# A hybrid transformer layer on eight cores: weight preparation moved into the first FFN, with smaller buffers

## The chip, the cores and the metric

One Trainium2 chip, 8 cores. Each core runs the same program on its own batch element (2048 tokens of width 1024); the cores do not talk to each other. The metric is the device time of the slowest core, in microseconds; smaller is better.

## What is computed

The reference is one layer of four sublayers, each added to its input after a LayerNorm without gain:

```python
x = x + mamba(_layernorm(x))      # D=1024, ED=2048, 16 states, conv of 15 taps
x = x + ffn(_layernorm(x))
x = x + block_attention(_layernorm(x))   # 16 heads, blocks of 64 tokens
x = x + ffn(_layernorm(x))        # the same weights again

def ffn(x, W1, b1, W2, b2, scale):       # H = 4096
    # m1, m2: products of 8 even and 8 odd early tokens (rank-one terms)
    h = x @ W1.T + scale * einsum('bsd,bhd->bsh', x, m1) + b1
    h = gelu(h)
    return h @ W2.T + scale * einsum('bsh,boh->bso', h, m2) + b2
```

W1 is 4096x1024 and W2 1024x4096, both fp32 in HBM. The kernel computes with bf16 copies, transposed so that the contraction lies on the partitions.

## The kernel before

The program is written as five lists of instructions, one for each engine (`te` TensorE, `ve` VectorE, `ac` ScalarE, `gp` GpSimd, `sy` SyncE). `Q.wait` puts a semaphore wait into a list, `inc` a semaphore increment behind an instruction. An engine works through its list in the order in which the Python code emitted it; nothing reorders it. Every operation is recorded through one helper, so the profile gives nearly all instructions line 57; they are told apart by tile. The profile leaves out digits in the names of buffers: `p_wnat`, `p_wnatB`, `p_wstage` and `p_ptp` are `p2_wnat`, `p2_wnatB`, `p2_wstage` and `p2_ptp` of `emit_prep2`.

The stages run one after the other: a prologue that transposes Win and Wout into DRAM scratch, `emit_mamba` (until a barrier on `st`, the semaphore of the writes to `s_x`), `emit_prep2`, `emit_ffn("a")`, `emit_attn`, `emit_ffn("b")`.

`emit_prep2` (from line 362) makes the transposed copies `s_W1T` and `s_W2T`, 32 rows of 128x1024 bf16 each. A row is done by `prep_row`: 8 transposes on TensorE into `p_ptp` (PSUM), one ScalarE copy into `p_wstage`, one SyncE DMA of 256 KB to DRAM. `p_ptp` and `p_wstage` have two slots, so row ci waits for the copy and the write of row ci-2. For W1, GpSimd loads a row of 128x1024 into one of two slots of `p_wnat`, once the transposes of row i-2 are done; these loads change fp32 to bf16 on the way. For W2, GpSimd issues 8 loads of 128x4096 into `p_wnatB` (64 KB of each partition), the tensor engine waits for all eight (`te.wait(lnb)`), and 32 rows follow. At the end SyncE waits for the last writes of both slots.

`emit_ln` loads four 128x1024 tiles through the two slots of `xres` (SyncE), takes the statistics on VectorE with a square root on ScalarE, normalizes into `xntok`, transposes on TensorE and copies into `xn_fm`.

`emit_ffn` first has SyncE issue 32 loads that bring all of `s_W2T` into SBUF (`f_w2a`, in the second FFN `f_w2b`; 64 KB of each partition), then `emit_ln` for the first quarter of the tokens. The tokens go in four quarters h. For h = 0, eight groups of transposes into `pRow` make the rows `ev1` and `ev4` for the rank-one terms. Then for each of 32 chunks c of H: SyncE loads `f_w1` (three slots) from `s_W1T`, 8 matmuls over the contraction and one of the rank-one term into `pA`, GELU on ScalarE into `f_h`. GpSimd carries small rows (`f_ufl`, `f_vfl`) from partitions 0 to 3 to partition 0. Then four tiles of 128 tokens are multiplied with `f_w2` (this is the first use of it, `te.wait(l_w2)`), and VectorE adds b2 and the residual, through `f_tx`.

The prologue has a relative of the W2 part, `prepB` for Wout: 8 loads of 128x2048 into `wnatB`, then rows with one PSUM tile `p_tp`, so that TensorE waits for ScalarE in every row. Its W1-like part loads Win into two slots `wnat`.

Of the kernel before, what the change touches and what calls it, by code (L numbers as in the profile page):

```python
# [7 lines left out]
F32 = mybir.dt.float32  # L8
BF16 = mybir.dt.bfloat16
# [4 lines left out]
D = 1024  # L14
# [92 lines left out]
def build_program(T=2048, nsub=4):  # L107
# [3 lines left out]
    nc = bass.Bass("TRN2", target_bir_lowering=False)  # L111
# [63 lines left out]
    b2_bc = b.sb("b2_bc", [128, D], F32)  # L175
# [187 lines left out]
    def emit_prep2():  # L363
        with contextlib.ExitStack() as prep:
            pb = lambda n, s, d: prep.enter_context(nc.sbuf_tensor(n, list(s), d))
            pps = lambda n, s, d: prep.enter_context(nc.psum_tensor(n, list(s), d))
            wnat = pb("p2_wnat", [128, 2, 1024], BF16)
            wnatB = pb("p2_wnatB", [128, 8, 4096], BF16)
            wstage = pb("p2_wstage", [128, 2, 1024], BF16)
            p_tp = pps("p2_ptp", [128, 2, 1024], BF16)  # L370
            ltp0 = b.sem("p2ltp0"); ltp1 = b.sem("p2ltp1"); ltpp = (ltp0, ltp1)
            lnb = b.sem("p2lnb")
            ttp = b.sem("p2ttp"); etp = b.sem("p2etp")
            wtp0 = b.sem("p2wtp0"); wtp1 = b.sem("p2wtp1"); wtpp = (wtp0, wtp1)
            tt_toks = []; et_toks = []; wb_toks = []

            def prep_row(ci, in_tile, cache_row):
                sl = ci % 2
                if ci >= 2:
                    te.wait(etp, et_toks[ci - 2])  # L380
                tok = None
                for k in range(8):
                    tok = te.transpose(out=p_tp[:, sl, k * 128:(k + 1) * 128],
                                       in_=in_tile[k],
                                       identity=eye[:, :])
                tok.inc(ttp, 8)
                tt_toks.append(ttp.n)
                ac.wait(ttp, tt_toks[ci])
                if ci >= 2:
                    ac.wait(wtpp[sl], wb_toks[ci - 2][1])  # L390
                ac.activation(out=wstage[:, sl, :], in_=p_tp[:, sl, :],
                              func=AF.Copy).inc(etp, 1)
                et_toks.append(etp.n)
                sy.wait(etp, et_toks[ci])
                sy.dma_start(out=cache_row, in_=wstage[:, sl, :]).inc(wtpp[sl], 16)
                wb_toks.append((wtpp[sl], wtpp[sl].n))

            ci = 0
            for i in range(32):
                sl = i % 2  # L400
                if i >= 2:
                    gp.wait(ttp, tt_toks[i - 2])
                gp.dma_start(out=wnat[:, sl, :],
                             in_=h_W1[i * 128:(i + 1) * 128, :]).inc(ltpp[sl], 16)
                te.wait(ltpp[sl])
                prep_row(ci, [wnat[:, sl, k * 128:(k + 1) * 128] for k in range(8)],
                         s_W1T[i, :, :])
                ci += 1
            for k in range(8):
                gp.dma_start(out=wnatB[:, k, :],  # L410
                             in_=h_W2[k * 128:(k + 1) * 128, :]).inc(lnb, 16)
            te.wait(lnb)
            for j in range(32):
                prep_row(ci, [wnatB[:, k, j * 128:(j + 1) * 128] for k in range(8)],
                         s_W2T[j, :, :])
                ci += 1
        return (wtp0, wtp1)

    def emit_ln(xsrc, tiles, xn_fm, kind, lnps_bf):
        for j, i in enumerate(tiles):  # L420
# [40 lines left out]
            if j == 0:  # L461
                te.wait(l_cv)
                te.wait(l_ox, l_ox.n)
            tok = None
            for k in range(8):
                tok = te.transpose(out=lnps_bf[:, k * 128:(k + 1) * 128],
# [360 lines left out]
                wout(h)  # L827
            barrier(st)

    def emit_ffn(tag, is_last):  # L830
        THF = T // 4
        NTHF = NT // 4
        fch = [(s0, min(512, THF - s0)) for s0 in range(0, THF, 512)]
        with contextlib.ExitStack() as fs:
# [9 lines left out]
            vfl = fb("f_vfl" + tag, [1, 16 * THF], BF16)  # L844
            vsb = fb("f_vsb" + tag, [4, THF], BF16)
            usb = fb("f_usb" + tag, [4, THF], BF16)
            ftx = fb("f_tx" + tag, [128, D], F32)
            pA = fs.enter_context(nc.psum_tensor("f_pA" + tag, [128, 2, 1024], F32))
            pR = fs.enter_context(nc.psum_tensor("f_pR" + tag, [4, 1024], F32))
            pRow = fs.enter_context(nc.psum_tensor("f_pRow" + tag, [1, 1024], BF16))  # L850
            pLN = fs.enter_context(nc.psum_tensor("f_pLN" + tag, [128, 1024], BF16))

            for k in range(32):
                sy.dma_start(out=w2a[:, k, :], in_=s_W2T[k, :, :]).inc(l_w2, 16)

            W1TOK = {}
            w1sem = (s_wzp[0], s_wzp[1], s_wzz[0])
            l_ev = emit_ln(s_x, list(range(NTHF)), xn_fm[:, 0, :, :], "plain", pLN[:, :])
            lntok = {0: l_ev.n}
            for h in range(4):  # L860
                xh = xn_fm[:, h % 2, :, :]
                te.wait(l_ev, lntok[h])
# [36 lines left out]
                for c in range(32):  # L899
                    sl = c % 2  # L900
                    sl3 = c % 3
                    if c >= 3:
                        sy.wait(s_q3, W1TOK[c - 3])
                    sy.dma_start(out=w1s[:, sl3, :], in_=s_W1T[c, :, :]).inc(w1sem[sl3], 16)
                    te.wait(w1sem[sl3])
                    if c >= 2:
                        te.wait(l_h, l_h.n - 1)
                    tok = None
                    for k in range(8):
                        for (t0, tw) in fch:  # L910
                            tok = te.matmul(out=pA[:, sl, t0:t0 + tw],
                                            lhsT=w1s[:, sl3, k * 128:(k + 1) * 128],
                                            rhs=xh[:, k, t0:t0 + tw],
                                            start=(k == 0), stop=False)
                    if c == 0:
                        te.wait(lg, lg.n)
                    ii = c // 8
                    for ti, (t0, tw) in enumerate(fch):
                        tok = te.matmul(out=pA[:, sl, t0:t0 + tw],
                                        lhsT=ev1[0:1, ii * 1024 + (c % 8) * 128:ii * 1024 + (c % 8) * 128 + 128],  # L920
                                        rhs=ufl[0:1, ii * THF + t0:ii * THF + t0 + tw],
                                        start=False, stop=True)
                    tok.inc(s_q3, 1)
                    W1TOK[c] = s_q3.n
                    ac.wait(s_q3)
                    ac.activation(out=hT[:, c, :], in_=pA[:, sl, 0:THF], func=AF.Gelu,
                                  bias=b1_fm[:, c:c + 1]).inc(l_h, 1)
                    if c % 8 == 7:
                        qi = c // 8
                        if qi == 0:  # L930
                            te.wait(s_q1, s_q1.n)
                        else:
                            te.wait(lg, lg.n)
                        te.wait(l_h, l_h.n)
                        tok = None
                        for k in range(8):
                            for (t0, tw) in fch:
                                tok = te.matmul(out=pR[:, t0:t0 + tw],
                                                lhsT=ltc[:, k, 9:16:2],
                                                rhs=hT[:, qi * 8 + k, t0:t0 + tw],  # L940
                                                start=(k == 0), stop=(k == 7))
                        tok.inc(l_v, 1)
                        ac.wait(l_v)
                        if qi >= 1:
                            ac.wait(lg, lg.n)
                        ac.activation(out=vsb[:, 0:THF], in_=pR[:, 0:THF],
                                      func=AF.Copy).inc(s_q4, 1)
                        gp.wait(s_q4)
                        for ii2 in range(4):
                            gp.dma_start(out=vfl[0:1, (qi * 4 + ii2) * THF:(qi * 4 + ii2 + 1) * THF],  # L950
                                         in_=vsb[ii2:ii2 + 1, 0:THF]).inc(lg, 16)
# [6 lines left out]
                for tt in range(NTHF):  # L958
# [13 lines left out]
                    for ii in range(4):  # L972
                        for qi in range(4):
# [3 lines left out]
                                            start=False, stop=(qi == 3 and ii % 2 == 1))  # L977
                    tok.inc(l_o, 1)
                    ve.wait(l_o); ve.wait(lxrp[sl])
                    ve.tensor_add(out=ftx[:, :], in0=xres[:, sl, :], in1=b2_bc[:, :])  # L980
                    ve.dr()
                    ve.tensor_add(out=xres[:, sl, :], in0=ftx[:, :],
                                  in1=pA[:, sl, 0:1024]).inc(l_ox, 1)
                    xr_used(sl, l_ox)
                    sy.wait(l_ox)
# [189 lines left out]
                barrier(st)  # L1175

    emit_mamba()
    p2sems = emit_prep2()
    sy.wait(p2sems[0]); sy.wait(p2sems[1])
    if nsub >= 2:  # L1180
        emit_ffn("a", is_last=(nsub == 2))
    if nsub >= 3:
        emit_attn()
    if nsub >= 4:
# [57 lines left out]
```

How the kernel before makes its waits and increments, by code:

```python
    def inc(self, sem, k=1):  # L41
        sem.n += k
        box = self.box
        self.q.rec.append(lambda e: box["i"].then_inc(sem.h, k))
        return self
# [21 lines left out]
    def wait(self, sem, n=None):  # L67
        v = sem.n if n is None else n
        if v > 0:
            self.rec.append(lambda e, v=v: e.wait_ge(sem.h, v))
```

## Time and profile before

| | us |
|---|---|
| median of 3 runs | 5758.94 |
| lowest and highest | 5660.82, 5759.61 |
| the profiled execution | 5649.85 |
| its span on the slowest core (core 3) | 5648.3 |
| spans of the 8 cores | 5614.4 to 5648.3 |

| engine | busy us | share of the span |
|---|---|---|
| PE (matmul) | 2743.2 | 49% |
| DVE (VectorE) | 2548.4 | 45% |
| ACT (ScalarE) | 1755.7 | 31% |
| POOL (GpSimd) | 399.9 | 7% |

The shares are averages over stages with different limits: the Mamba stage (until about 3291 us) is bound by the scans on VectorE, the two FFN (about 3577 to 4297 and 4924 to 5648 us) by TensorE. The mean granted clock of TensorE is 0.725 to 0.729 on all cores. In the rows below, a time is in microseconds from the first instruction, "x8" is the number of instructions merged into a row, and the brackets hold the idle time of the engine before it and what ended it. Landing is the time from the issue of a DMA to its semaphore.

### The profile page before, as it was taken

How to read it: one execution, taken by the hardware profiler on the slowest of the kernel's cores; microseconds unless marked ns; L12 is line 12 of the kernel's file. 1: busy time of each engine (PE TensorE's matmuls, PEld its weight loads, DVE VectorE, ACT ScalarE, POOL GpSimd, SP SyncE). 2: the span in 40 equal slices, each digit the busy share in tenths (PEclk: the TensorE clock that was granted, in tenths of full speed). 3: DMA queues.
4: the chain of work that ended last, by engine and by line, in shares of the span. 5: the costliest groups of instructions: out<-in, count | busy, mean ns of one | idle time of the engine just before them, and what ended most of it. 6: DMA issues, size and time to landing. Idle time of an engine off the chain costs nothing.

```text
span 5648.3 us, 41604 instructions; the slowest of 8 cores (5614.4 to 5648.3 us)
## 1 busy us (share of the span) xinstructions
PE 2743.2 (49%) x12960; PEld 1202.1 (21%) x12960; DVE 2548.4 (45%) x2198; ACT 1755.7 (31%) x2562; POOL 399.9 (7%) x378
## 2 busy tenths in 40 slices
PE   3352333323333233332222322698896544398988
PEld 2220111101111111111000111233332322233333
DVE  0106999249996299990999610101101333210010
ACT  2213555125553055540555322311111222212111
POOL 1140111001110001110000010000000000000000
PEclk9985666666666666666565755888997666588889
DMA  7412000320001400004000167322224111322221
GB/s 118 102 38 43 19 19 19 52 80 19 19 21 25 112 13 20 19 16 97 20 12 14 56 131 186 97 73 73 83 75 93 58 62 56 119 75 90 84 73 64
DMA packets 202301, 345.40 MB, mean 61 GB/s; under 512 B 49924, under 2 KB 86916, under 8 KB 201060
## 3 DMA queue, kind: packets, MB, share of 16 engines
q1 hardware_dynamic: 173990, 289.47, 17.8%
q0 software_dynamic: 28096, 53.27, 5.6%
q8 instruction: 109, 1.79, 0.1%
q14 instruction: 106, 0.87, 0.1%
HBM read 301.06 MB, written 71.45 MB: 66 GB/s over the span
## 4 chain that ended last, share of the span: by engine, by line
PE 33%; DVE 27%; issue 10%; DMA 10%; DVEq 8%; ACT 5%; SPq 5%; POOL 1%; another core or an unknown queue 1%; ACTq 0%; POOLq 0%
DVE m_hall L57 15%; PE f_pAb L57 11%; PE f_pAa L57 10%; DVEq L73 8%; DVE m_dBall L57 5%; SPq L57 5%; PE a_pA L57 3%; PE m_pB L57 3%; DVE m_txd L57 2%; DMA m_yfr<-s_yfc 2%; DMA xres<-x 1%; DMA p_wnat<-W 1%; PE m_pA L57 1%; POOL m_diag L57 1%; DMA xres<-s_x 1%
## 5 line engine op out<-in xcount | busy, mean ns | idle before, releaser
L57 DVE TENSOR_TENSOR_SCAN m_hall<-m_dA,carry,m_dBall 128x512 bf16<-128x512 f32 x1024 | 1342.8, 1385 | 11.9 <-issue 11.0
L57 PE MATMUL m_pB<-m_gall,eye 128*128 128x512 bf16 x1024 | 365.4, 535 | 1428.8 <-DVE m_gall L57 1428.8
L57 ACT ACTIVATE m_dA<-m_delta,A_fm 128x512 f32<-128x512 f32 x1024 | 731.9, 721 | 949.8 <-DVE m_hall L57 854.2
L57 DVE BATCH_NORM_STATS2 stat<-xres 128x6 f32<-128x512 f32 x128 | 82.0, 683 | 1073.7 <-DMA xres<-s_x 854.5
L57 PEld LDWEIGHTS m_pB<-m_gall,eye 128*128 128x128 bf16 x1024 | 128.0, 129 | 1654.6 <-issue 1626.0
L57 ACT ACT_TABLE_LOAD x158 | 202.7, 1283 | 768.0 <-DVE r1a L57 387.9
L57 POOL TENSOR_TENSOR m_diag<-convw_fm,eye 128x1920 bf16<-128x1920 f32 x64 | 240.4, 3756 | 1417.2 <-PE m_pB L57 1417.2
L57 DVE TENSOR_TENSOR m_dBall<-m_dxb,m_bcB 128x8192 bf16<-128x8192 bf16 x64 | 283.2, 4425 | 5.9
L57 DVE TENSOR_TENSOR m_gall<-m_hall,m_bcC 128x8192 bf16<-128x8192 bf16 x64 | 283.2, 4425 | 0.6 <-issue 0.6
L57 PE MATMUL f_pAb<-f_w2b,f_hb 128*128 128x512 bf16 x1024 | 258.1, 419 | 4.5 <-DMA f_vflb<-f_vsbb 4.5
L57 PE MATMUL f_pAb<-f_xnb,f_w1b 128*128 128x512 bf16 x1024 | 253.1, 392 | 9.6 <-DMA f_w1b<-s_W1T 9.6
L57 PE MATMUL f_pAa<-f_xna,f_w1a 128*128 128x512 bf16 x1024 | 251.6, 390 | 10.6 <-DMA f_w1a<-s_W1T 10.5
L57 PE MATMUL f_pAa<-f_w2a,f_ha 128*128 128x512 bf16 x1024 | 251.2, 411 | 4.5 <-DMA f_vfla<-f_vsba 4.5
L57 PE MATMUL m_pB<-m_xinp,m_diag 128*128 128x512 bf16 x960 | 230.6, 394 | 46.0 <-POOL m_diag L57 46.0
L57 DVE TENSOR_SCALAR m_txd<-xres,mu,r1a 128x1024 f32<-128x1024 f32 x16 | 16.5, 1033 | 492.0 <-DMA xres<-x 367.4
L57 DVE TENSOR_TENSOR f_txb<-xres,b_bc 128x1024 f32<-128x1024 f32 x16 | 19.6, 1226 | 381.7 <-PE f_pAb L57 381.7
L57 DVE TENSOR_TENSOR f_txa<-xres,b_bc 128x1024 f32<-128x1024 f32 x16 | 19.6, 1226 | 374.9 <-PE f_pAa L57 374.9
L57 PE MATMUL m_pA<-m_wouta,m_yfr 128*128 128x512 bf16 x256 | 72.4, 409 | 230.7 <-DMA m_yfr<-s_yfc 230.3
L57 ACT ACTIVATE f_ha<-f_pAa,b_fm 128x512 bf16<-128x512 f32 x128 | 87.9, 687 | 181.4 <-PE f_pAa L57 181.4
L57 ACT ACTIVATE f_hb<-f_pAb,b_fm 128x512 bf16<-128x512 f32 x128 | 87.9, 687 | 181.3 <-PE f_pAb L57 181.3
L57 ACT ACTIVATE p_wstage<-p_ptp 128x1024 bf16<-128x1024 bf16 x64 | 64.7, 1023 | 248.6 <-PE p_ptp L57 231.7
L57 PEld LDWEIGHTS f_pAb<-f_w2b,f_hb 128*128 128x128 bf16 x1024 | 107.7, 106 | 153.1 <-issue 55.7
(154 smaller groups left out, 3456.5 us busy)
## 6 DMA issues: line engine op xcount, KB each, us to landing
xres<-s_x SPq DMA_DIRECT2D x96, 512.0 KB, 3.3
f_w1a<-s_W1T SPq DMA_DIRECT2D x128, 256.0 KB, 2.6
f_w1b<-s_W1T SPq DMA_DIRECT2D x128, 256.0 KB, 2.6
s_x<-xres SPq DMA_DIRECT2D x48, 512.0 KB
xres<-x SPq DMA_DIRECT2D x32, 512.0 KB, 3.7
m_wz<-s_WinT POOLq DMA_DIRECT2D x64, 256.0 KB, 2.9
m_wzz<-s_WinT SPq DMA_DIRECT2D x64, 256.0 KB, 2.7
m_wouta<-s_WoutT SPq DMA_DIRECT2D x64, 256.0 KB, 2.6
```

Source lines behind the costliest of these rows:

```text
L57: box["i"] = getattr(e, fname)(*a, **kw)
L73: self.rec.append(lambda e: e.drain())
```

## The change

- `emit_prep2` is no longer called between the stages. `emit_ffn("a")` calls it as `prep_hook`, after its first `emit_ln` has been emitted. To let it live beside the FFN's buffers it is made smaller: one slot of `p_wnat`, `p_wnatB` of 512 columns, one slot of `p_ptp`.
- A row now waits for the copy of the row before, and a W1 load for the transposes of the row before. W2 goes in eight pieces: 8 loads of 128x512, then 4 rows; the loads of a piece wait for the last transposes before it.
- The loads of `f_w2` move from SyncE, ahead of `emit_ln`, to GpSimd, behind `emit_ln` and the hook; in the first FFN each waits for the write of its row. The second FFN has no hook. SyncE waits for each W1 row before it loads it, for h = 0.
- `pRow` becomes a part of `pLN`, with a wait on `s_q1` in `emit_ln`; `f_tx` goes, the sum is formed in `xres`.

```diff
-            wnat = pb("p2_wnat", [128, 2, 1024], BF16)
-            wnatB = pb("p2_wnatB", [128, 8, 4096], BF16)
+            wnat = pb("p2_wnat", [128, 1, 1024], BF16)
+            wnatB = pb("p2_wnatB", [128, 8, 512], BF16)
...
-            p_tp = pps("p2_ptp", [128, 2, 1024], BF16)
+            p_tp = pps("p2_ptp", [128, 1024], BF16)
...
-                if ci >= 2:
-                    te.wait(etp, et_toks[ci - 2])
+                if ci >= 1:
+                    te.wait(etp, et_toks[ci - 1])
...
-                if i >= 2:
-                    gp.wait(ttp, tt_toks[i - 2])
-                gp.dma_start(out=wnat[:, sl, :],
+                if i >= 1:
+                    gp.wait(ttp, tt_toks[i - 1])
+                gp.dma_start(out=wnat[:, 0, :],
...
-            for k in range(8):
-                gp.dma_start(out=wnatB[:, k, :],
-                             in_=h_W2[k * 128:(k + 1) * 128, :]).inc(lnb, 16)
-            te.wait(lnb)
-            for j in range(32):
...
+            for quar in range(8):
+                gp.wait(ttp, tt_toks[ci - 1])
+                for k in range(8):
+                    gp.dma_start(out=wnatB[:, k, :],
+                                 in_=h_W2[k * 128:(k + 1) * 128,
+                                          quar * 512:(quar + 1) * 512]).inc(lnb, 16)
+                te.wait(lnb, lnb.n)
+                for j in range(4):
...
+        return (wb_toks[0:32], wb_toks[32:64])
...
                 te.wait(l_ox, l_ox.n)
+                te.wait(s_q1, s_q1.n)
...
-            ftx = fb("f_tx" + tag, [128, D], F32)
...
-            pRow = fs.enter_context(nc.psum_tensor("f_pRow" + tag, [1, 1024], BF16))
             pLN = fs.enter_context(nc.psum_tensor("f_pLN" + tag, [128, 1024], BF16))
-
-            for k in range(32):
-                sy.dma_start(out=w2a[:, k, :], in_=s_W2T[k, :, :]).inc(l_w2, 16)
+            pRow = pLN[0:1, :]
...
             lntok = {0: l_ev.n}
+            ptoks = prep_hook() if prep_hook is not None else None
+            for k in range(32):
+                if ptoks is not None:
+                    gp.wait(ptoks[1][k][0], ptoks[1][k][1])
+                gp.dma_start(out=w2a[:, k, :], in_=s_W2T[k, :, :]).inc(l_w2, 16)
...
                         sy.wait(s_q3, W1TOK[c - 3])
+                    if ptoks is not None and h == 0:
+                        sy.wait(ptoks[0][c][0], ptoks[0][c][1])
...
-                    ve.tensor_add(out=ftx[:, :], in0=xres[:, sl, :], in1=b2_bc[:, :])
+                    ve.tensor_add(out=xres[:, sl, :], in0=xres[:, sl, :], in1=b2_bc[:, :])
...
-    p2sems = emit_prep2()
-    sy.wait(p2sems[0]); sy.wait(p2sems[1])
     if nsub >= 2:
-        emit_ffn("a", is_last=(nsub == 2))
+        emit_ffn("a", is_last=(nsub == 2), prep_hook=emit_prep2)
```

## Rows read from the trace of the kernel before

**Rows 1.** The page: span; granted TensorE clock in 40 slices (tenths)

```profile
span 5648.3 us, 41604 instructions; the slowest of 8 cores (5614.4 to 5648.3 us)
...
PEclk9985666666666666666565755888997666588889
```

**Rows 2.** Windows: start:end, length, busy us (instructions) PE, PEld, DVE, ACT, POOL; PEclk, DMA share, GB/s

```profile
3291.00:3402.00 111.00, 32.38 (x256) 24.77 (x256) 0.00 (x0) 31.71 (x31) 21.02 (x40) 0.50 0.79 152
3402.00:3449.00 47.00, 0.00 (x0) 0.00 (x0) 0.00 (x0) 1.02 (x1) 0.00 (x0) 0.50 0.99 177
...
3505.00:3554.00 49.00, 4.05 (x32) 3.10 (x32) 10.69 (x29) 5.85 (x9) 0.00 (x0) 0.50 0.69 231
...
3577.00:3675.00 98.00, 80.17 (x353) 30.88 (x352) 10.62 (x28) 31.06 (x46) 9.72 (x20) 0.93 0.34 105
```

**Rows 3.** Chain that ended last: start us, length us, what held it

```profile
3401.01 48.13 another core or an unknown queue
3524.86 10.93 DMA xres<-s_x
```

**Rows 4.** Timeline, W1 rows: start us, us, engine, operation [idle before <-releaser]

```profile
3290.81 1.12 POOL L57 DMA_DIRECT2D p_wnat<-W  x2 [748.53 <-DMA s_x<-xres]
...
3302.44 1.01 PE L57 MATMUL p_ptp<-eye,p_wnat 128*128 128x128 bf16 x8 [4.50 <-DMA p_wnat<-W]
...
3304.00 0.53 POOL L57 DMA_DIRECT2D p_wnat<-W  x1 [4.98 <-PE p_ptp L57]
```

**Rows 5.** Landing of the p_wnat loads, issue to landing

```profile
DMA to landing us min/median/max: 4.3/4.7/6.6
```

**Rows 6.** The same for the loads wnat of the first weight (Win)

```profile
DMA to landing us min/median/max: 4.4/4.5/6.9
```

**Rows 7.** The same for POOL loads without type change (m_wz, 256 KB)

```profile
DMA to landing us min/median/max: 2.7/2.9/5.0
```

**Rows 8.** POOL queue, 3300 to 3390 us: packets, MB, share of 16 engines

```profile
q0 software_dynamic: 3886, 7.08, 59.8%
```

**Rows 9.** The same, 3405 to 3448 us (W2 load)

```profile
q0 software_dynamic: 1016, 7.35, 98.5%
```

**Rows 10.** The same, 158 to 184 us (Wout load)

```profile
q0 software_dynamic: 1102, 4.03, 99.0%
```

**Rows 11.** Timeline of POOL: the Wout load is issued

```profile
153.78 4.23 POOL L57 DMA_DIRECT2D wnatB<-Wout  x8 [6.39 <-PE p_tp L57]
```

**Rows 12.** Timeline of the Wout rows (one PSUM buffer)

```profile
185.36 1.01 PE L57 MATMUL p_tp<-eye,wnatB 128*128 128x128 bf16 x8 [29.64 <-DMA wnatB<-Wout]
...
187.69 1.01 PE L57 MATMUL p_tp<-eye,wnatB 128*128 128x128 bf16 x8 [1.32 <-ACT wstage L57]
```

**Rows 13.** Timeline of the W2 rows (two PSUM buffers)

```profile
3449.38 1.87 PE L57 MATMUL p_ptp<-eye,p_wnatB 128*128 128x128 bf16 x16 [48.37 <-DMA p_wnatB<-W]
...
3454.90 1.93 PE L57 MATMUL p_ptp<-eye,p_wnatB 128*128 128x128 bf16 x16 [1.27 <-ACT p_wstage L57]
```

**Rows 14.** Timeline, start of the first FFN

```profile
3505.32 19.39 SPq L57 DMA_DIRECT2D f_w2a<-s_W2T  x32
...
3535.89 1.29 DVE L57 BATCH_NORM_STATS2 stat<-xres 128x6 f32<-128x512 f32 x2 [248.32 <-DMA xres<-s_x]
...
3551.61 1.01 PE L57 MATMUL f_pLNa<-eye,xntok 128*128 128x128 bf16 x8 [2.45 <-DVE xntok L57]
...
3554.29 1.01 PE L57 MATMUL f_pRowa<-eye,f_ltca 128*1 128x128 bf16 x8 [1.67 <-DVE f_ltca L57]
```

**Rows 15.** Timeline, start of the second FFN

```profile
4848.07 20.27 SPq L57 DMA_DIRECT2D f_w2b<-s_W2T  x32
4868.50 19.18 SPq L57 DMA_DIRECT2D xres<-s_x  x4
4879.05 1.29 DVE L57 BATCH_NORM_STATS2 stat<-xres 128x6 f32<-128x512 f32 x2 [33.73 <-DMA xres<-s_x]
```

**Rows 16.** The page, part 6: issues, KB each, median us to landing

```profile
xres<-s_x SPq DMA_DIRECT2D x96, 512.0 KB, 3.3
```

More of the change, by code:

```diff
@@ L378, in prep_row @@
                 sl = ci % 2
-                if ci >= 2:
-                    te.wait(etp, et_toks[ci - 2])
+                if ci >= 1:
+                    te.wait(etp, et_toks[ci - 1])
                 tok = None
                 for k in range(8):
-                    tok = te.transpose(out=p_tp[:, sl, k * 128:(k + 1) * 128],
+                    tok = te.transpose(out=p_tp[:, k * 128:(k + 1) * 128],
                                        in_=in_tile[k],
@@ L390, in prep_row @@
                     ac.wait(wtpp[sl], wb_toks[ci - 2][1])
-                ac.activation(out=wstage[:, sl, :], in_=p_tp[:, sl, :],
+                ac.activation(out=wstage[:, sl, :], in_=p_tp[:, :],
                               func=AF.Copy).inc(etp, 1)
@@ L399, in emit_prep2 @@
             for i in range(32):
-                sl = i % 2
-                if i >= 2:
-                    gp.wait(ttp, tt_toks[i - 2])
-                gp.dma_start(out=wnat[:, sl, :],
-                             in_=h_W1[i * 128:(i + 1) * 128, :]).inc(ltpp[sl], 16)
-                te.wait(ltpp[sl])
-                prep_row(ci, [wnat[:, sl, k * 128:(k + 1) * 128] for k in range(8)],
+                if i >= 1:
+                    gp.wait(ttp, tt_toks[i - 1])
+                gp.dma_start(out=wnat[:, 0, :],
+                             in_=h_W1[i * 128:(i + 1) * 128, :]).inc(ltpp[i % 2], 16)
+                te.wait(ltpp[i % 2])
+                prep_row(ci, [wnat[:, 0, k * 128:(k + 1) * 128] for k in range(8)],
                          s_W1T[i, :, :])
                 ci += 1
-            for k in range(8):
-                gp.dma_start(out=wnatB[:, k, :],
-                             in_=h_W2[k * 128:(k + 1) * 128, :]).inc(lnb, 16)
-            te.wait(lnb)
-            for j in range(32):
[L414 to L417, printed above, removed]
+            for quar in range(8):
[6 more added lines that the diff above has]
+                for j in range(4):
+                    prep_row(ci, [wnatB[:, k, j * 128:(j + 1) * 128] for k in range(8)],
+                             s_W2T[quar * 4 + j, :, :])
+                    ci += 1
+        return (wb_toks[0:32], wb_toks[32:64])
     def emit_ln(xsrc, tiles, xn_fm, kind, lnps_bf):
@@ L828, in emit_mamba, with emit_ffn @@
             barrier(st)
-    def emit_ffn(tag, is_last):
+    def emit_ffn(tag, is_last, prep_hook=None):
         THF = T // 4
@@ L979, in emit_ffn @@
                     ve.wait(l_o); ve.wait(lxrp[sl])
-                    ve.tensor_add(out=ftx[:, :], in0=xres[:, sl, :], in1=b2_bc[:, :])
+                    ve.tensor_add(out=xres[:, sl, :], in0=xres[:, sl, :], in1=b2_bc[:, :])
                     ve.dr()
-                    ve.tensor_add(out=xres[:, sl, :], in0=ftx[:, :],
+                    ve.tensor_add(out=xres[:, sl, :], in0=xres[:, sl, :],
                                   in1=pA[:, sl, 0:1024]).inc(l_ox, 1)
@@ L1177, in build_program @@
     emit_mamba()
-    p2sems = emit_prep2()
-    sy.wait(p2sems[0]); sy.wait(p2sems[1])
     if nsub >= 2:
-        emit_ffn("a", is_last=(nsub == 2))
+        emit_ffn("a", is_last=(nsub == 2), prep_hook=emit_prep2)
+    else:
+        emit_prep2()
     if nsub >= 3:
```

## The prediction, made before the changed kernel was timed

> **What bounds the kernel now.** I read the page first: the busy shares of the engines, the granted clock by slice and the chain, which show a program of stages one after the other. The change touches none of the scans of the Mamba stage and none of the FFN's matrix loops; it touches the passage between them, 3290 to 3577 us, and the start of the second FFN, from 4848 us. In the passage TensorE runs at its lower level, 1.2 GHz (PEclk 0.50), and idles more than it works; in the FFN it is granted 0.93 [rows 1, 2]. So I asked the windows, the chain and the timeline of that passage what each row waits for.
>
> Three things bound it. In the W1 part PE is busy 32.4 of 111 us and the DMA engines 0.79: each row of W1 waits for its load [rows 2]. Then all of W2 is loaded in one piece; the chain holds it as one step of 48.1 us, with the DMA engines at 0.99 [rows 2, 3]. The 32 W2 rows that follow go in pairs, four of them in 3454.90 - 3449.38 = 5.5 us [rows 13]. At last SP issues 32 loads of f_w2a in 19.4 us before it issues the first load of the LayerNorm, which then takes 10.9 us to land behind them [rows 3, 14]. From POOL's first W1 load (3290.81) to the first transpose into pRow (3554.29) it is 263.5 us [rows 4, 14]. I predict this stretch anew, and the start of the second FFN.
>
> **The change part by part.**
>
> *Order.* The hook stands in emit_ffn, but each engine runs its own list in order. PE gets the 4 LayerNorm groups, then all 64 rows of prep, then the first FFN's work; ACT and SP likewise. No FFN matmul can run under prep. What can overlap is one W1 load with the LayerNorm, and the w2a loads with the end of prep.
>
> *LayerNorm first, +20.4 us ahead of prep.* Its load is issued at about 3290.8, when the barrier opens, and lands in 3.3 us [rows 16]; from the first statistics to the fourth group of transposes it is 3551.61 - 3535.89 = 15.7 us [rows 14]; its 8 transposes take 1.0 us. 3.3 + 15.7 + 1.0 = 20.0, with 0.4 for issue. Row 0 of W1 begins at 3311.2; its load, issued at 3290.8, is hidden under this.
>
> *W1 with one wnat buffer.* The next load may be issued only when the row's transposes are done. From the start of a row's transposes to the load that they release it is 3304.00 - 3302.44 = 1.56 us [rows 4]. The load took 4.3 / 4.7 / 6.6 us with mostly two in flight [rows 5], 4.4 / 4.5 / 6.9 for Win, where loads overlap less [rows 6]. Now one is in flight alone: I take 4.4, and 0.1 until PE starts. Period 6.1 us (5.95 at the minimum; 6.9 at 5.2). 31 periods are 189.1 us, so the last row starts at 3500.3. The SP write-back and the ACT copy of a row end inside 6.1 us, so the single PSUM buffer costs nothing here.
>
> *W2 rows with one PSUM buffer.* PE must wait for ACT after each row. The Wout rows of the prologue have just this form: 187.69 - 185.36 = 2.33 us a row [rows 12]. Four rows start within 3 x 2.33 = 7.0 us.
>
> *W2 in eight pieces.* Each piece is 8 loads of 128x512, 1 MB as bf16 against 8 MB before, and its issue waits until the last transpose of the piece before. So nothing of it is hidden. No row shows such a piece; I bound it. By bytes: one 256 KB load lands in 4.5 us [rows 6], the Wout load, 8 x 512 KB, took from 153.78 to 185.36, 31.6 us [rows 11, 12]; the line through both gives 1 MB at 9.9. By packets: POOL's queue used 90 x 16 x 0.598 / 3886 = 222 ns of an engine for a packet of W1 (2 KB runs), 43 x 16 x 0.985 / 1016 = 667 ns for W2 (8 KB), 26 x 16 x 0.99 / 1102 = 374 ns for Wout (4 KB) [rows 8, 9, 10]. Halving the run takes off 293, then 152 ns, next perhaps 76: 146 ns for the new 1 KB runs. A piece has 1024 of them and 128 small ones, 72 for each engine: 10.5 us, and 2.5 us of start and end (4.5 less nine packets of 222 ns), together 13.0. I take 12, nearer to packets. Lower end 8.5 (W2's own rate, 5.9 us per MB, and 2.5); upper end 18 (1 KB runs cost what 2 KB runs do, 72 x 222 ns = 16.0, and 2.5, rounded). A piece then takes 1.56 + 12 + 7.0 = 20.6 us, eight take 164.5, and the last row starts at 3664.8. PE is free for pRow 1.0 us later, at 3665.8, against 3554.3: +111.5 us. From there the first FFN runs as before.
>
> *w2a on POOL.* 32 issues, 0.58 us each at most, of which 28 can go out under the last piece's transfers and rows; POOL is done at about 3669 and is next wanted for f_ufl at about 3690. That is the cover; if it fails, f_ufl waits some us. In the first FFN the 19.4 us of SP issue and the slow LayerNorm load are thus gone, which the sum above holds already, since nothing of them stands in it.
>
> *Second FFN, gain.* Its LayerNorm load is issued at 4868.50, behind 20.3 us of w2b issues, and DVE starts at 4879.05 [rows 15]. Now both start at 4848.1 on two queues. The bounds: DVE starts 3.3 us later if the load is undisturbed (27.5 us gained), or the load fares as if behind the w2b stream (0). The DMA engines share, and the later LayerNorm loads meet the stream too: I take 22.
> The page "DMA: Bandwidth & Descriptors" of the Trainium skill (Issuing engines are not separate DMA queues) says that a second issuing engine saves only the time on the sequencer. By that the gain is the 20.3 us of issue; the sum would be 2 us higher.
>
> *At nothing:* pRow as a part of pLN with its wait on s_q1 (the count is reached when xntok is), the add into xres instead of ftx (the same shape), and the waits of SP on write-backs long landed. Clock: PE idles longer, at the level it already has.
>
> **Sum.** +111.5 - 22 = +89.5 us on the profiled execution, 5649.85 us by its own time (span 5648.3): 5739 us, 1.6% more. The median of the runs shown is 5758.94, 109 us above that execution, their lowest 5660.82: the same sum on the median is 5848, one more reason for a high upper end.
>
> A rule that speaks otherwise: the Trainium skill, "DMA: Bandwidth & Descriptors" (Anatomy of one DMA), puts a POOL load at about 2.0 us and its bytes over 436 GB/s. For 256 KB that is 2.6 us; this trace has at least 4.3 [rows 5], so it disagrees for these loads, which change type on the way. By the Trainium skill's page W1 would take 31 x 4.3 us and a piece about 6, and the kernel would end near 5634.
>
> **The rivals.**
> A, the pieces are dear (slower by over 2%). The 1 KB runs cost nearly what the 2 KB runs do. From 15 us a piece the total passes 5763 (+24 us in eight pieces). For it: the price of a packet falls more slowly than its bytes at each halving [rows 8 to 10]; eight starts and ends. Against: it falls at each. At 17 us: 5779; with lone loads of 5.2 us as well: about 5800.
> B, a lone load is quick (not slower, the other side). The 4.5 us might be mostly a queue of two. POOL's plain loads of 256 KB landed in 2.9 us [rows 7]. Then W1's period is 4.56 and takes 141.4; a piece takes 3.7 of issue and 2.9, 6.6, eight 121.3. 20.4 + 141.4 + 121.3 + 1.0 = 284.1, +20.6, less 22: 5648. It decides from about 3 us a load. Against: the minimum of 64 loads that change type is 4.3 us [rows 5, 6].
> The formula of the Trainium skill's page "DMA: Bandwidth & Descriptors" (Anatomy of one DMA) amounts to much the same.
> C, prep is hidden under the FFN after all. Then over 200 us go, 5430. The order of PE's list forbids it.
>
> **How the numbers follow.** Forecast (about +90, 5700 to 5790): 0.60. A: 0.28. B: 0.09. C: 0.03. The low end of the forecast is 4.3 us a load, 8.5 a piece and 27.5 gained: 5701. The high ends together (5.2, 18, no gain) give 5834. The range 5690 to 5850 leaves out B, C and a little on top. Over 2% or not is about what a measurement can tell: faster 0.03 (C), within 2% (below 5763) 0.65 (most of the forecast, and B), slower 0.32 (A and the forecast's upper part).
>
> **What would show it.** In the profile after: the W1 rows of p_ptp 6.1 us apart, with POOL released by PE in each; eight waits of PE for p_wnatB, about 12 us each, where one of 48 us stood; rows 2.33 us apart between them; the passage from barrier to pRow about 375 us long; w2a issued from POOL with no wait on the path; DVE of the second FFN at about 4854 on the old time scale. Wrong would be: loads under 3.5 us, pieces over 15 us or under 8, FFN matmuls between prep rows, f_ufl late behind w2a, or another clock in the FFN.

## The result, and the profile after

| | before | after |
|---|---|---|
| median of all executions (10 and 10) | 5671.03 us | 5819.35 us |
| lowest, highest | 5635.53, 5782.31 us | 5736.12, 5876.94 us |
| the profiled execution | 5649.85 us | 5744.98 us |
| its span | 5648.3 us | 5743.4 us |

The ratio of after to before is 1.0181, with a 95% interval of 1.012 to 1.0242: the change made the kernel slower by about 1.8%, and the interval leaves open whether it is more than 2%. The executions of either kernel lie on two levels some 100 us apart, whatever the kernel, so the ratio is taken between executions on the lower level, and the medians of the table, which mix the two, say less.

The page of the kernel after, its span and the granted clock:

```profile
span 5743.4 us, 41755 instructions; the slowest of 8 cores (5696.7 to 5743.4 us)
...
PEclk9985666656666666666666655689897667698888
```

After the prologue the clock stands at 5 and 6 tenths until the first FFN, much as before (5 to 7 tenths [rows 1]); only the FFN begins later.

The W1 rows in the timeline of the kernel after (start us, us, engine, operation, idle time before it and what ended it):

```profile
3313.29 1.06 PE L57 MATMUL p_ptp<-eye,p_wnat 128*128 128x128 bf16 x8
...
3319.84 1.01 PE L57 MATMUL p_ptp<-eye,p_wnat 128*128 128x128 bf16 x8 [5.49 <-DMA p_wnat<-W]
...
3321.39 0.53 POOL L57 DMA_DIRECT2D p_wnat<-W  x1 [5.96 <-PE p_ptp L57]
...
3325.99 1.01 PE L57 MATMUL p_ptp<-eye,p_wnat 128*128 128x128 bf16 x8 [5.14 <-DMA p_wnat<-W]
...
3327.54 0.53 POOL L57 DMA_DIRECT2D p_wnat<-W  x1 [5.62 <-PE p_ptp L57]
```

A row every 6.2 us, and POOL waits 5.6 us for PE before each load: load and transposes take turns. Before, two loads were in flight, and POOL was held for the row before the last [rows 4]. The landing of these loads, from the tile's view:

```profile
DMA to landing us min/median/max: 4.2/4.4/7.6
```

The median is 4.4 us alone against 4.7 with two in flight [rows 5].

The W2 part in the chain that ended last (start us, length us, what):

```profile
3508.63 3.64 POOL p_wnatB L57 x7
3512.27 6.07 DMA p_wnatB<-W
...
3645.86 9.04 DMA p_wnatB<-W
3659.74 7.70 DMA s_W2T<-p_wstage
```

Where one load of 48.1 us stood in the chain [rows 3], there are eight issues of 3 to 4 us with 5 to 9 us of landing behind each. Two pieces and the end of prep in the timeline (PEld is the weight load of TensorE; the last row is the first transpose of pRow):

```profile
3518.58 1.01 PE L57 MATMUL p_ptp<-eye,p_wnatB 128*128 128x128 bf16 x8 [10.50 <-DMA p_wnatB<-W]
...
3520.91 1.01 PE L57 MATMUL p_ptp<-eye,p_wnatB 128*128 128x128 bf16 x8 [1.32 <-ACT p_wstage L57]
...
3537.53 1.01 PE L57 MATMUL p_ptp<-eye,p_wnatB 128*128 128x128 bf16 x8 [10.94 <-DMA p_wnatB<-W]
...
3646.39 14.96 POOL L57 DMA_DIRECT2D f_w2a<-s_W2T  x28
...
3655.15 1.01 PE L57 MATMUL p_ptp<-eye,p_wnatB 128*128 128x128 bf16 x8 [13.47 <-DMA p_wnatB<-W]
...
3665.04 1.02 ACT L57 ACTIVATE p_wstage<-p_ptp 128x1024 bf16<-128x1024 bf16 x1 [5.37 <-DMA s_W2T<-p_wstage]
...
3667.15 0.72 PEld L57 LDWEIGHTS f_pLNa<-eye,f_ltca 128*1 128x1 bf16 x8 [0.20 <-issue]
```

The first piece took 3518.58 - 3508.63 = 9.95 us, the rows come 2.33 us apart, as in the Wout part [rows 12]. The last piece took 12.9 us (3655.15 - 3642.22, its first issue), because POOL sends 28 loads of f_w2a right behind it (3646.39); they also hold up a write-back, for which ACT waits 5.4 us at 3665.04.

The start of the second FFN:

```profile
4962.63 14.25 SPq L57 DMA_DIRECT2D xres<-s_x  x4
4963.01 6.96 POOL L57 DMA_DIRECT2D f_w2b<-s_W2T  x13 [546.66 <-DMA s_x<-xres]
4968.03 1.29 DVE L57 BATCH_NORM_STATS2 stat<-xres 128x6 f32<-128x512 f32 x2 [8.27 <-DMA xres<-s_x]
...
4991.70 1.01 PE L57 MATMUL f_pLNb<-eye,f_ltcb 128*1 128x128 bf16 x8 [1.67 <-DVE f_ltcb L57]
```

SP and POOL start within 0.4 us, VectorE follows 5.4 us after the issue of its load, and pRow is reached after 4991.70 - 4962.63 = 29.1 us, where it was 49.4 us (4848.07 to 4897.47; the start is in [rows 15]).

The difference of the two profiled executions, 95.1 us of span, is made up so: the passage, from POOL's first W1 load to pRow, is 3667.15 - 3291.40 = 375.8 us against 263.5, +112.3; the second FFN's start -20.3; everything else +3.1.

### The profile page after: what moved, and what is told of

Same layout as the page of the kernel before. It is cut to its first block, busy times and chain, and to the rows that moved or that the text cites. A ratio compares the mean times of both kernels' runs of the same rounds, so it can differ in the third digit from the quotient of the medians.

```text
span 5743.4 us, 41755 instructions; the slowest of 8 cores (5696.7 to 5743.4 us)
## 1 busy us (share of the span) xinstructions
PE 2736.9 (48%) x12960; PEld 1199.9 (21%) x12960; DVE 2548.3 (44%) x2198; ACT 1756.9 (31%) x2562; POOL 462.2 (8%) x498
## 4 chain that ended last, share of the span: by engine, by line
PE 33%; DVE 27%; DMA 11%; issue 11%; DVEq 8%; ACT 5%; SPq 4%; POOL 2%; ACTq 0%; POOLq 0%
DVE m_hall L57 15%; PE f_pAb L57 10%; PE f_pAa L57 10%; DVEq L73 7%; DVE m_dBall L57 5%; SPq L57 4%; PE a_pA L57 3%; PE m_pB L57 3%; DMA p_wnat<-W 2%; DVE m_txd L57 2%; DMA m_yfr<-s_yfc 2%; DMA xres<-x 1%; PE m_pA L57 1%; PE p_ptp L57 1%; POOL m_diag L57 1%
## 5 line engine op out<-in xcount | busy, mean ns | idle before, releaser
L57 DVE TENSOR_TENSOR xres<-xres,b_bc 128x1024 f32<-128x1024 f32 x32 | 39.2, 1225 | 757.1 <-PE f_pAa L57 379.4
L57 PEld LDWEIGHTS f_pAa<-f_w2a,f_ha 128*128 128x128 bf16 x1024 | 106.7, 105 | 150.0 <-issue 50.4
```

Of the source, the lines that this page charges most:

```text
L57: box["i"] = getattr(e, fname)(*a, **kw)
```

## The experiments

Each of the runs below is read by its trace: the passage by stages, with the stretch from the first to the last transpose of PE for W1, from there to the last transpose for W2, and to pRow. Before these are 105, 100 and 53 us, after they are 194, 159 and 0.3 (the LayerNorm, 20 to 22 us, now stands in front).

**One slot of p_wnat, alone**, in the kernel before.

```diff
-            wnat = pb("p2_wnat", [128, 2, 1024], BF16)
+            wnat = pb("p2_wnat", [128, 1, 1024], BF16)
...
-                if i >= 2:
-                    gp.wait(ttp, tt_toks[i - 2])
+                if i >= 1:
+                    gp.wait(ttp, tt_toks[i - 1])
...
```

> The kernel before with one slot of p_wnat and nothing else changed. Theory (costs add, each wait is serial): the W1 rows come 6.2 us apart where they came 3.4 apart, 31 periods are 89 us more, the W2 part is unchanged; the profiled time is about 5739. Rival (the loss of the change comes from prep standing behind the LayerNorm in the first FFN, not from its buffers): the W1 rows stay under 4 us apart and the time is within 20 us of before.

The tile p_ptp: engine, operation, count, durations, first and last start:

```profile
L57 PE MATMUL p_ptp<-eye,p_wnat x256: 263/311/314, 3299.6 to 3494.8; 128*128 128x128 bf16 x128
```

195 us for 31 periods: the whole loss of the W1 part comes from this slot, wherever prep stands. The passage was 358.2 us, 95 more. The time was 5745.4 us, 96 above before on the same chip (5649.63; one execution of each).

**One slot of p_ptp, alone.**

```diff
-            p_tp = pps("p2_ptp", [128, 2, 1024], BF16)
+            p_tp = pps("p2_ptp", [128, 1024], BF16)
...
-                if ci >= 2:
-                    te.wait(etp, et_toks[ci - 2])
+                if ci >= 1:
+                    te.wait(etp, et_toks[ci - 1])
...
```

> The kernel before with one slot of p_ptp. Theory: nothing in the W1 part, whose rows wait for loads; the W2 rows go from 1.6 to 2.33 us apart, 31 of them are +21.5 us; about 5671. Rival (PE waits for ACT in the W1 part too): the W1 rows lengthen by up to 1 us each, 30 us more.

```profile
L57 PE MATMUL p_ptp<-eye,p_wnat x256: 263/311/314, 3302.6 to 3409.0; 128*128 128x128 bf16 x128
...
L57 PE MATMUL p_ptp<-eye,p_wnatB x256: 265/314/314, 3458.8 to 3533.6; 128*128 128x128 bf16 x128
```

The W1 rows take 106 us, as before; the W2 rows take 74.8 us from first to last start, where they took 51.4 (3449.4 to 3500.8). +23 us there, and the passage is 288.7 us, +25. Of its two times, 5676.2 and 5835.3 us, the profiled one is the lower. The rival on the W1 part is out.

**Eight pieces, alone**, with both slots of p_ptp.

```diff
-            wnatB = pb("p2_wnatB", [128, 8, 4096], BF16)
+            wnatB = pb("p2_wnatB", [128, 8, 512], BF16)
...
+            for quar in range(8):
+                gp.wait(ttp, tt_toks[ci - 1])
...
```

> The kernel before with W2 in eight pieces, two slots of p_ptp kept. Theory: a piece is 1.6 us until its issue, 10.4 us of load and 3.5 us until its fourth row starts, 15.5 in all, 124 us for eight where 100 stood: +24, about 5674. The rival that the pieces are dear because of their short runs: loads of 15 us or more, +60 us.

```profile
3397.79 4.24 POOL L57 DMA_DIRECT2D p_wnatB<-W  x8 [6.72 <-PE p_ptp L57]
...
3409.14 1.86 PE L57 MATMUL p_ptp<-eye,p_wnatB 128*128 128x128 bf16 x16 [11.90 <-DMA p_wnatB<-W]
...
3413.95 4.24 POOL L57 DMA_DIRECT2D p_wnatB<-W  x8 [11.92 <-PE p_ptp L57]
...
3424.20 1.86 PE L57 MATMUL p_ptp<-eye,p_wnatB 128*128 128x128 bf16 x16 [10.79 <-DMA p_wnatB<-W]
```

Pieces of 11.4 and 10.3 us, 15.1 us from piece to piece (3424.20 - 3409.14); the last W2 row starts 125 us after the last W1 row, against 100. The time was 5668.6, +19. A piece isn't dear: my rival A falls.

**The loads of f_w2 on POOL, alone**: the gaining half of the change, in the kernel before.

```diff
             for k in range(32):
-                sy.dma_start(out=w2a[:, k, :], in_=s_W2T[k, :, :]).inc(l_w2, 16)
+                gp.dma_start(out=w2a[:, k, :], in_=s_W2T[k, :, :]).inc(l_w2, 16)
...
     sy.wait(p2sems[0]); sy.wait(p2sems[1])
+    gp.wait(p2sems[0]); gp.wait(p2sems[1])
```

> The kernel before with the 32 loads of f_w2 issued by POOL, in both FFN (in the first POOL waits for the last write-backs first). Theory: this is the gaining half of the change: 20 us at the second FFN as in the changed kernel, and about 20 at the first, where VectorE starts the LayerNorm some 5 us after the issue where it took 30, and the LayerNorm runs 5 us longer beside the stream; about 5610. Rival (the DMA engines are shared, so nothing is gained at the first FFN): 20 us in all, 5630.

Its three executions took 5720.7, 5760.6 and 5813.9 us where 5610 was expected, so the time of this run shows no gain. In the profiled one cores 4 and 5 had a granted clock of 0.71, where before has 0.725 to 0.729 on all cores; I read core 3, at 0.729, whose span was 5598.3 us. Start of the first FFN there:

```profile
3502.73 13.52 SPq L57 DMA_DIRECT2D xres<-s_x  x4
3503.09 4.81 POOL L57 DMA_DIRECT2D f_w2a<-s_W2T  x9 [109.02 <-DMA s_W2T<-p_wstage]
3507.19 1.29 DVE L57 BATCH_NORM_STATS2 stat<-xres 128x6 f32<-128x512 f32 x2 [223.61 <-DMA xres<-s_x]
```

VectorE starts 4.5 us after the issue of its load, where it started 30.6 us after SP's first w2a issue [rows 14]; from the last W2 row to pRow it is 33.6 us against 53.5, and the second FFN's start takes 28.9 against 49.4. Together 40 us in the stretches that the loads stand in. Timed by itself:

> The kernel before with the loads of f_w2 on POOL, timed. The undisturbed cores of its profile were 40 to 45 us shorter than before: the theory expects a ratio of 0.992 to 0.994. Rival: no gain, 1.00.

The ratio was 0.9979, interval 0.9935 to 1.0023: about 12 us, less than expected. No gain at all is not excluded by it, but 40 us on the slowest core are just outside (the interval ends at 37). The typical core did gain: in the executions behind the ratio the median of the eight cores was 5592.5 to 5609.7 us, where it was 5629.2 to 5651.6 before, some 35 us less. In the trace of this run both stretches are short again on every core that I read, but on its slowest core, core 6, the last stretch from pRow took 762.8 us, where core 3 of before took 750.8; from the second matrix phase on, the products with f_w2b, the granted clock was 0.86 there against 0.88. Why the slowest core gives back most of the 40 us is open; in the kernel after, where the same loads were moved, that stretch stayed level (751.7).

**Two slots of p_wnat in the kernel after.**

```diff
-            wnat = pb("p2_wnat", [128, 1, 1024], BF16)
+            wnat = pb("p2_wnat", [128, 2, 1024], BF16)
...
-                if i >= 1:
-                    gp.wait(ttp, tt_toks[i - 1])
+                if i >= 2:
+                    gp.wait(ttp, tt_toks[i - 2])
...
```

> The changed kernel with two slots of p_wnat, which undoes that one part. Theory: the W1 rows return to 3.4 us apart, -88 us: about 5655, level with before. Rival (placement costs): a gain under 40 us.

The first execution profiled had TensorE at 0.70 on all cores and took 5823.5 us, far from the 5655 expected; its passage was 284.5 us, 91 less. It was repeated:

> The changed kernel with two slots of p_wnat once more, since the execution profiled before ran at a lower clock in all its stages outside prep. Theory: the passage is 285 us as then, the rest as in the changed kernel, about 5655. Rival: the quicker passage is paid back in the FFN or the attention, over 5700.

```profile
L57 PE MATMUL p_ptp<-eye,p_wnat x256: 262/311/314, 3313.5 to 3417.5; 128*128 128x128 bf16 x128
...
L57 PE MATMUL p_ptp<-eye,p_wnatB x256: 262/314/314, 3428.5 to 3577.7; 128*128 128x128 bf16 x128
```

104 us of W1 rows, a passage of 284.7 us and a time of 5658.8: 86 us less than after, and level with before: the passage is 21.2 us longer than before, and the second FFN's start 20.4 us shorter (4907.9 - 4878.9 = 29.0). So the place of prep, the pieces and the single p_ptp cost, together, no more than the moved loads give back; the 90 us of this slot are the loss that is seen.

**What a lone load is made of.**

```diff
-                             in_=h_W1[i * 128:(i + 1) * 128, :]).inc(ltpp[i % 2], 16)
+                             in_=s_WinT[i, :, :]).inc(ltpp[i % 2], 16)
```

> The changed kernel, with the W1 rows read from the bf16 scratch of Win instead of from W1, so the load keeps its type and reads half the bytes; the FFN is so computed with other weights. Theory (the time of a lone load is its transfer with change of type on top of a start): a load lands in 2.9 us as m_wz did, the rows come 4.6 us apart, -51 us: about 5694. Rival (a lone load costs 4.4 us whatever it carries, start and end): 6.2 us apart, no change.

```profile
L57 PE MATMUL p_ptp<-eye,p_wnat x256: 263/311/314, 3311.7 to 3469.1; 128*128 128x128 bf16 x128
...
DMA to landing us min/median/max: 2.9/3.3/4.8
```

The load of bf16 rows, half the bytes and no change of type, lands in 3.3 us, and the rows come 157.4 / 31 = 5.1 us apart, not 4.6. The time was 5709.2 us, 36 less than after, where the theory had 51 and the rival nothing. I had carried 2.9 us over from m_wz and was 0.4 short; the theory holds in kind, but most of a lone load's time is left when the bytes are halved. Of the 6.2 us of a period about 1.1 are the other half of the bytes and the change of type, 3.3 what even this load takes, 1.6 the transposes and the way back to POOL.

**f_w2a held back.**

```diff
                 if ptoks is not None:
-                    gp.wait(ptoks[1][k][0], ptoks[1][k][1])
+                    gp.wait(ptoks[1][30][0], ptoks[1][30][1])
+                    gp.wait(ptoks[1][31][0], ptoks[1][31][1])
```

> The changed kernel with the f_w2a loads held back until the last two write-backs of prep have landed. Theory (the stream of w2a slows the last piece and the last write-backs): the last piece loads in 10.4 us where it took 12.9, and the 5 us stall of ScalarE before the last but one row goes; 5 to 7 us less in the passage. Rival (they are then in the way of f_ufl and f_w1a): as much is lost after it; the sum is within 3 us.

PE's waits on core 0 of this run, between 3640 and 3780 us (us in total, times, longest):

```profile
PE f_pAa L57 <- DMA f_ufla<-f_usba: 7.8, 1, 7.8
...
PE p_ptp L57 <- ACT p_wstage L57: 4.0, 3, 1.3
```

The stall of ACT is gone, the last piece took 10.3 us on core 6 where it took 12.9, and the passage is 3.2 to 8.3 us shorter (367.5 to 370.3 against 373.5 to 375.8, cores 6 and 0 against 3 and 1). But f_ufl now queues behind f_w2a on POOL's queue, and PE waits 7.8 us for it (11.4 on core 6), where it waited 2.5; the stretch from the first product with f_w1a to the second matrix phase takes 106.0 and 110.1 us on cores 0 and 6, where it took 98.4 and 99.9 on cores 1 and 3 of after. In its first 20 us the granted clock was 0.81 and 0.63, where it was 1.00 and 0.87. The rival was right: it is paid back, and somewhat more. The time was even 5765.4 us, 20 above after; most of that lies behind the second matrix phase, on core 6 at a mean granted clock of 0.719, and no run explains it. This is the cover that the prediction named, a few us wide.

**Two pieces instead of eight**, into the free buffer f_ha.

```diff
-            for quar in range(8):
+            for quar in range(2):
...
-                    gp.dma_start(out=wnatB[:, k, :],
+                    gp.dma_start(out=hT[:, 4 * k:4 * k + 4, :].rearrange("p a b -> p (a b)"),
...
-                                          quar * 512:(quar + 1) * 512]).inc(lnb, 16)
+                                          quar * 2048:(quar + 1) * 2048]).inc(lnb, 16)
```

> The changed kernel with W2 loaded in two pieces of 2048 columns, into the buffer f_ha, which is free during prep. Theory: a piece is now 4 MB with runs of 4 KB and takes between 26 and 31.6 us (the Wout load); the W2 part is 2 x (1.6 + 26 to 31.6 + 35) = 125 to 136 us where 152 to 159 stood: -15 to -30 us. If a piece of 1 MB was mostly start and end (7 us or more of its 10.4), the gain is over 35 us.

```profile
3513.31 3.64 POOL f_ha L57 x7
3516.95 25.72 DMA f_ha<-W
3579.47 2.99 POOL f_ha L57 x6
3583.11 26.45 DMA f_ha<-W
```

A piece of 4 MB takes 29.4 us (3.64 + 25.72), four times the bytes for 2.8 times the time of a piece of 1 MB. The stretch from the last W1 to the last W2 row is 138.8 us, 20 less, within what was expected. The time was 5727.95.

**Prep inside the first quarter of the first FFN.** The runs say that the loss is serial waiting for loads while PE works 32 us in each part and the DMA engines are half idle (shares of 0.47 and 0.59 in the W1 and W2 parts of the kernel after). The remedy is to have loads in flight under work that must be done anyway.

```diff
                 for c in range(32):
...
+                    if inl:
+                        if c + 1 < 32:
+                            row1(c + 1)
+                        te.wait(et1, E1[c])
...
+                    if inl:
+                        row2(c)
```

`row1` has the 8 transposes of a W1 row, the copy into its slot of f_w1, the write to s_W1T and the load of the row four further on; between it and `row2` stand the matmuls and the GELU of chunk c; `row2` transposes a W2 row into pLN, copies it into f_w2a and writes s_W2T. The buffers of this version: four slots of p_wnat, two pieces of W2 (one of its own, one in the second half of f_xn, which is free then), no p_wstage.

> A new version, built on what the earlier runs showed: prep is taken apart and stands inside the 32 chunks of the first quarter of the first FFN. Chunk c transposes W1 row c+1 and copies it straight into its f_w1 slot, multiplies chunk c, transposes W2 row c and copies it straight into f_w2a; SyncE writes both to the scratch for later use. The loads of W1 go four rows ahead, those of W2 one to two pieces ahead, all issued by POOL; w2b is loaded by POOL as in the change. Theory: the loads are no longer waited for singly, the reload of f_w2a and the first reading of s_W1T go, and the stretch is bound by the DMA engines (32 x about 5 us: 1.8 + 1.8 us for loads of one row each, 1.4 for two writes); from the barrier to the second matrix phase of that quarter it is 22 + 22 + 160 to 170 = about 210 us where 384 stood (263.5 + 22.5 + 98.2), and with 20 us at the second FFN the kernel takes 5450 to 5470. Rival: in each chunk PE waits for a copy of ACT (serial chain of two transposes, two copies and the matmuls, 6.5 us or more), then the stretch is 250 us or more and the kernel over 5490.

Windows of core 5 (start:end, length, busy us (instructions) of PE, PEld, DVE, ACT, POOL; PEclk, DMA share, GB/s):

```profile
3290.00:3312.00 22.00, 1.01 (x8) 0.77 (x8) 8.95 (x17) 2.15 (x3) 10.85 (x20) 0.50 0.60 131
...
3336.00:3500.00 164.00, 121.72 (x843) 62.88 (x841) 0.00 (x0) 87.08 (x102) 48.06 (x92) 0.83 0.88 180
```

The DMA engines are at 0.88 while PE works 121.7 of 164 us. From the barrier to the second matrix phase it is 3527.0 - 3299.6 = 227 us, where it was 384, 17 more than expected: the early loads of W1 and W2 stand in the way of the LayerNorm's (its third tile landed after 10.9 us), and pRow came 30.9 us after the barrier, not 22. The 32 chunks took 171 us. The profiled execution took 5473.94. Timed:

> The inlined version, timed against the kernel before. From its one profiled execution, 5474: the theory expects a ratio of 0.965 to 0.975 to before. Rival: the denser work of the first quarter lowers the granted clock later, or the single execution was a lucky one, and the ratio is 0.98 or more.

The ratio to before was 0.9706, interval 0.9655 to 0.9756 (medians 5479.56 and 5656.3). This version beats both kernels.

## Why the prediction failed, and where it held

The working gave +89.5 us, a ratio of 1.016; measured were +95.1 us between the profiled executions and a ratio of 1.018. Still the predicted number was wrong, and the step that failed is the last of the **Sum**. It set the number on the level of the profiled execution, 5739 us, beside a stated median of 5758.94 for before. Read against that median, 5739 is a gain of 0.3%, the other way than the whole argument. The text saw it (it gave 5848 for the same sum on the median) and used it only to stretch the range. On its own level the sum was only 6 us low: the profiled execution of after took 5744.98 us. The gap between the lowest and the median of the runs shown, 1.7%, is as large as the effect; a forecast of a change must be put as a ratio, and its number worked out from the same median that it will be read against: 5758.94 x 1.0158 = 5850. The ten executions since put the median of before at 5671.03 and that of after at 5819.35, 80 us above the number; it lies inside the range because the range was stretched for the median, not because of the sum.

Term by term:

| step | predicted | measured |
|---|---|---|
| LayerNorm ahead of prep | +20.4 | 21.9 (3313.29 - 3291.40) |
| 31 periods of W1 | 189.1 | 193.8 |
| W2 to its last row | 164.5 | 159.1 |
| last row to pRow | 1.0 | 0.9 |
| passage against 263.5 | +111.5 | +112.3 |
| start of the second FFN | -22 | -20.3 |
| all else | 0 | +3.1 |
| sum | +89.5 | +95.1 |

- *Order.* It held: no FFN matmul stands between prep rows, and rival C is out.
- *LayerNorm.* 1.5 us short. VectorE started 5.6 us after SP's issue, not 3.3. Its load shared the DMA engines with the first W1 load, which landed after 7.6 us where 4.4 is the median, and with the second LayerNorm load; no run tells the two apart.
- *W1.* The period is 6.25 us, not 6.1: a landing of 4.4 us as taken, but 4.6 from issue to PE and 1.6 back, and a few slower loads. The experiment with one slot alone puts the whole term where the prediction put it.
- *W2 pieces.* Without the stall of 4.1 us, a piece took (159.1 - 4.1 - 8 x 8.6) / 8 = 10.8 us on average, not 12. The price of the packets failed: POOL's queue used 80 x 16 x 0.372 / 4608 = 103 ns of an engine for one, not 146, by the line below. The series 293, 152, 76 ns did not go on: by it the step to 1 KB runs should have taken off 76 ns, and it took off 119 from 222.

The same view as [rows 8 to 10], of the kernel after from 3560 to 3640 us (W2 pieces), and then from 3320 to 3500 us (W1 rows):

```profile
q0 software_dynamic: 4608, 4.20, 37.2%
```

```profile
q0 software_dynamic: 4162, 7.59, 36.9%
```

- *The stall* was not in the sum: the stream of f_w2a was costed at nothing on the path, and made PE wait 5.4 us for ACT where 1.3 are usual, and the last piece 2 to 3 us longer. Two errors, the piece and the stall, went against each other, so that the term came out within 5.4 us partly by luck.
- *The second FFN* held within 2 us. The Trainium skill, "DMA: Bandwidth & Descriptors" (Issuing engines are not separate DMA queues), says that a second issuing engine saves the sequencer's time alone; the 20.3 us measured are just the 20.3 us of SP issue, so here the traces agree.
- *Rival A* (dear pieces): out, 10 to 13 us. *Rival B* (a quick lone load) is out: no load of W1 landed under 3.9 us in the traces of before, of after and of the kernel before with one slot. Nor does the formula of the Trainium skill's page "DMA: Bandwidth & Descriptors" (Anatomy of one DMA) hold here: an estimate by it is 2.6 us for 256 KB, against 3.3 us for the plain load with one in flight and 4.4 us for the one that changes type; the loads m_wz come nearest, from 2.7 us, with a median of 2.9 [rows 7].
- *Clock.* Held: 0.50 in prep, and 0.93 in the FFN's first chunks, from 3690 to 3788 us of the kernel after.

## What to carry to other kernels

Moving a stage "inside" another on engines that work in order hides nothing unless its instructions stand between the other's; buffers cut to make room for the move can cost more than the move gives. A loop whose next load waits for the last use of its only buffer pays load, use and the way back in turn: here 6.2 us a row where two slots gave 3.4. And put a forecast as a ratio on the median it will be read against; the terms can all be right and the number still point the wrong way.

## What the runs showed of the hardware that was not expected

- A POOL load of 128x1024 with one in flight landed in 4.4 us (fp32 to bf16, 512 KB read) and in 3.3 us (bf16, 256 KB read): three quarters of the time stay when half the bytes and the change of type go.
- Runs of 1 KB were not dear: 103 ns of an engine for each packet of POOL's queue, against 222 ns for 2 KB runs with mostly two loads in flight, and 180 x 16 x 0.369 / 4162 = 255 ns with one.
- The clock of TensorE rose from 0.50 to 0.83 when prep was interleaved with the FFN, without a loss after it (in the second FFN's matrix phases 0.89, against 0.88 before); TensorE's transposes took 216 to 219 ns there, where they took 311 ns in prep by itself.
